# A two-layer adaptive-norm and expert network on one core: each step of the four middle stages gets its own place in its engine's order

## The chip, the core and the metric

One Trainium2 chip, of which one core is used. The metric is the device time of one execution of the whole program, in microseconds (us). Five engines each work through a list of instructions of their own, in the order in which the list was written: TensorE (PE in the profile; PEld is its weight load), VectorE (DVE), ScalarE (ACT), GpSimd (POOL) and SyncE (SP, which here only issues DMAs). An instruction that has to wait for a semaphore holds up everything behind it on its engine. So the order of each list is a large part of the program, and the change is one of order alone.

## What is computed

The input x is 8 x 256 tokens of 128 numbers. Two layers are applied, each with a residual; cut to what matters:

```python
x = x + L0_ffn(L0_cond(x, W1, b1, v, type_ids), gate_weight, w1, b1, w2, b2)
x = x + L1_ffn(L1_cond(x, language_ids, W1, b1, W2, b2, gamma, beta), ...)

# L0_cond: masked softmax pooling over a prefix, a postfix or all but one of the tokens
# L0_ffn: 8 experts, every token through every expert
kth_val = jnp.sort(logits.reshape(-1))[expert_k - 1]
gates = logits * (logits >= kth_val)
h = gelu_tanh(einsum('bld,ehd->bleh', x, w1) + b1)
out = einsum('bld e,ble->bld', einsum('bleh,edh->blde', h, w2) + b2.T, gates)

# L1_cond: adapter of the sample's language, then layernorm with its gamma and beta
h = relu(x @ W1[lang] + b1[lang]);  x = layernorm(x + h @ W2[lang] + b2[lang])
# L1_ffn: layernorm, softmax over 8 experts, the best 2 of them, exact gelu
w, idx = top_k(softmax(xn @ gate_w), 2);  w = w / sum(w)
output = sum over the 2 chosen experts of w * (gelu(xn @ w1[e] + b1[e]) @ w2[e] + b2[e])
return output + residual
```

The first expert layer is dense (8 experts for 2048 tokens, hidden width 512). The second is sparse: only 2 of 8 experts are computed for a token.

## The kernel before, in words

**Units.** The matmul work is cut into 88 units. Units 0 to 63 are dense (first layer): 16 steps of two (expert, group) parts, four hidden chunks each, where a group is 512 tokens (four groups, 0 to 3). Units 64 to 87 are pairs of tiles (second layer): a tile is 128 rows of tokens that chose one expert. Tiles 0 to 30 are batch 0 (tokens of groups 0, 1 and 2), tiles 31 to 45 are batch 1 (group 3). Each unit goes PE (first product, `pe_m1`, lines 533 to 562) to ACT (gelu, `act_gelu`, L627 and L632) to ACT (high half, `hi_part`, L649) to DVE (low half, `lo_part`, L656) to PE (second product, `pe_m2`, L596 and L597 for tiles, L606 to L608 for dense units). The operands are float16 in a high and a low half, so that each product is three matmuls.

**Gated sums.** For a dense result `gated` (L708, four instructions) adds it, times the gate, to the accumulator of its group. The gates come from a bisection of 12 rounds on DVE and PE (L1152 to L1193), and so the first ten results are kept in SBUF.

**Middle stages.** When a group's dense sums are complete, `mid(g)` (lines 1244 to 1580) takes it through 31 steps, each at its place among the units' instructions. In order of dependence, with the names of the table: `x1T` transpose on PE and `x1c` its copy on ACT; `h` and `hr`, `ad` and `xa`, the adapter; `st1`, `rs1`, `n1`, `x2`, the first layernorm (L1305 and L1310 statistics on DVE, L1329 and L1330 reciprocal root on POOL, L1338 and L1349 on DVE); `st2`, `rs2`, `n2`, `xn`, the second (L1362, L1370); `hi` (L1381) and `lo` (L1386) split the rows; `nT`, `nTc`, `lg`, the router's logits (L1393, L1400, L1408); `top`, the two best experts (L1419 to L1459); `tanh`, `wk`, their weights; `rk` and `rkd`, the rank of each row within its expert (L1522 to L1541, the last one writes the row addresses `idx`); `sc`, eight indirect DMAs on POOL (L1552) that scatter the group's rows to the DRAM buffer `sorted_in`; `gd`, `gT`, `gTc`, `b2m`, `b2x`, the bias of the second expert layer; `acc`, the residual (L728).

**Tiles.** When all groups of a batch are scattered and the tile table (L1605 to L1637) is there, SP loads each tile's rows (`sp_in`, L1662, with row addresses read from the table), PE transposes them (`pe_t`, L1692), ACT (batch 0) or DVE (batch 1) copies them out of PSUM, and DVE computes the rows' destination (`dve_xe`, L1727 and L1730). Results go through DVE (`dve_y`, L1718) and one indirect DMA for each tile on POOL (`pool_out`, L1669) to `sorted_out`. At the end SP loads the results back in token order and DVE adds them (`add_moe`, L746, four instructions for each group and choice), and SP stores (L1763).

**The order.** Every step is put into the list of its engine with a position, a number; each list is then sorted by it. Dense unit u stands at position 2u (a position is about 1.32 us), tile pairs `TILE` apart. A middle step's position is the group's start `M0[g]` plus an offset from the table `MID`, stretched by `SLACK`:

```python
def mid_pos(name, g):
    return M0[g] + (MID[name] + SLACK[g] * HOPS[name]) / UNIT_US
...
at("act", upos[u] + 0.7 * uwid[u], hi_part(u))
at("dve", upos[u] + 1.4 * uwid[u], lo_part(u))
...
at("dve", m2_pos(US + n, len(tiles) - 1) + 0.9, dve_y)
at("dve", mpos[("t", n)] + 0.8, dve_xe)
...
for q in Q.values():
    q.sort(key=lambda x: (x[0], x[1]))
```

`W16POS` says where the split of the second layer's weights into halves stands for each of the 8 experts (`w16_high` on ACT, L804, and `w16_low` on DVE, L811). In what follows a step of a group is written as name(group): `x2(2)` is the step `x2` of group 2.

Of the kernel before, what the change touches and what calls it, by code (L numbers as in the profile page):

```python
# [61 lines left out]
TILE = [1.45, 1.35]  # L62
GAP = 2.0
SLACK = [0.8, 0.8, 0.4, 0.0]

MID = {
# [17 lines left out]
W16POS = [3.0, 7.0, 11.0, 66.0, 71.0, 76.0, 81.0, 86.0]  # L84
# [3 lines left out]
def build_adaln_ffn(nc, t, out):  # L88
# [69 lines left out]
    with ExitStack() as ctx:  # L158
# [276 lines left out]
        M0 = [max(pos for pos, k, v in terms if group_of(k, v) == g) + 1.0 for g in range(NG)]
        M0[0] += 1.0
        M0[1] = max(M0[1], M0[0] + 9.0)
        M0[2] = max(M0[2], M0[1] + 7.0)
# [1487 lines left out]
```

## Time and profile before

| | |
|---|---|
| median of 3 runs | 424.14 us (422.88 to 426.02) |
| the profiled execution, its own time | 423.4 us |
| its span, first to last instruction | 421.6 us |
| mean granted TensorE clock | 0.908 |
| matmuls | 3474 |

The profile is of one execution. "Busy" is the time in which an engine runs an instruction. In a timeline row the first number is the start in us from the start of the span, the second how long the row lasts; "x4" means that four instructions are merged in it, and a bracket at the end gives the idle time of the engine ahead of it and who ended it. "issue" there means that nothing the profile shows ended the idle time. The granted clock is a share of full speed: 1.00 is 2.4 GHz, 0.50 is 1.2 GHz.

### The profile page before, as it was taken

To read this page: it belongs to the slowest core of one execution; us is meant where nothing else is said; L and a number is where in the kernel's file an instruction comes from. 1 tells how busy PE (TensorE), PEld (TensorE's weight loads), DVE (VectorE), ACT (ScalarE), POOL (GpSimd) and SP (SyncE) were. 2 spreads that over 40 slices of the span, in tenths; PEclk is the share of its full clock that TensorE was granted. 3 is DMA by queue.
4 is the path that set the end of the run, shared out by engine and by line. 5 is a ranking of instruction groups with operands and counts; after the bars stand their busy time and mean duration, and the time that the engine had idled before them with its cause. 6 is when DMAs were issued, how large, how long until landed. Compare 5 with 4: busy or idle time off the path is not lost.

```text
span 421.6 us, 9890 instructions
## 1 busy us (share of the span) xinstructions
PE 352.1 (84%) x3474; PEld 254.3 (60%) x3474; DVE 286.5 (68%) x796; ACT 241.9 (57%) x312; POOL 96.8 (23%) x100
## 2 busy tenths in 40 slices
PE   8988988999999998989579969149997898888920
PEld 5645865777776675757456647028675666666710
DVE  1754459988998666899978698513658844546672
ACT  3463287778887587987467656206355426633510
POOL 0000000000000000132146810700144577443440
PEclk9656699999999999999899998759988989999985
DMA  6892003326920203314001100121111222226132
GB/s 211 289 304 93 2 1 101 84 59 200 328 83 2 90 2 100 113 63 128 1 21 34 53 0 2 45 57 27 39 53 40 59 65 75 67 67 184 37 100 87
DMA packets 25762, 35.42 MB, mean 84 GB/s; under 512 B 6740, under 2 KB 21348, under 8 KB 25332
## 3 DMA queue, kind: packets, MB, share of 16 engines
q1 hardware_dynamic: 22900, 29.51, 23.7%
q0 software_dynamic: 2496, 5.15, 3.7%
q8 instruction: 30, 0.49, 0.5%
q10 hardware_dynamic: 320, 0.13, 0.1%
q14 instruction: 16, 0.13, 0.1%
HBM read 28.59 MB, written 15.64 MB: 105 GB/s over the span
## 4 chain that ended last, share of the span: by engine, by line
PE 44%; DVE 18%; issue 17%; POOL 10%; SPq 5%; DMA 4%; ACT 1%; POOLq 0%; DVEq 0%; ACTq 0%
POOL sorted_in L1552 4%; PE bank L606 4%; PE psA L559 4%; PE psA L561 4%; PE bank L607 4%; PE psA L560 4%; PE bank L608 4%; POOL sorted_out L1669 4%; DVE l L656 4%; PE bank L596 2%; DVE acc L708 2%; PE bank L995 2%; PE psA L544 2%; PE psA L540 2%; DVE w L811 2%
## 5 line engine op out<-in xcount | busy, mean ns | idle before, releaser
L656 DVE SCALAR_TENSOR_TENSOR l<-h 128x1024 f16<-128x1024 f32 x88 | 106.1, 1206 | 42.7 <-ACT h L649 42.5
L632 ACT ACTIVATE h<-psA,b1f 128x512 f32<-128x512 f32 (+1 forms) x96 | 76.0, 826 | 63.1 <-PE psA L561 62.6
L606 PE MATMUL bank<-w,h 128*128 128x128 f16 x512 | 92.7, 223 | 6.0 <-DVE acc L708 6.0
L649 ACT ACTIVATE h<-h 128x1024 f16<-128x1024 f32 x88 | 92.0, 1045 | 1.5
L607 PE MATMUL bank<-w,h 128*128 128x128 f16 x512 | 92.5, 223 | 0.0
L608 PE MATMUL bank<-w,l 128*128 128x128 f16 x512 | 92.4, 223 | 0.0
L1669 POOL DMA_INDIRECT sorted_out<-w,xe x46 | 46.9, 1019 | 77.5 <-DVE w L1718 35.7
L606 PEld LDWEIGHTS bank<-w,h 128*128 128x128 f16 x512 | 51.3, 100 | 17.0 <-DVE acc L708 9.7
L607 PEld LDWEIGHTS bank<-w,h 128*128 128x128 f16 x512 | 51.1, 100 | 6.0 <-issue 0.6
L627 ACT ACTIVATE h<-psA 128x1024 f32<-128x1024 f32 (+1 forms) x24 | 23.7, 988 | 53.4 <-PE psA L546 51.8
L608 PEld LDWEIGHTS bank<-w,l 128*128 128x128 f16 x512 | 51.2, 100 | 0.0
L1329 POOL TENSOR_SCALAR rs<-mv 128x4 f32<-128x4 f32 x8 | 4.6, 577 | 199.0 <-DVE mv L1310 198.9
L561 PE MATMUL psA<-xh,w 128*128 128x512 f16 x128 | 49.5, 387 | 0.0
L559 PE MATMUL psA<-xh,w 128*128 128x512 f16 x128 | 49.5, 386 | 0.0
L560 PE MATMUL psA<-xl,w 128*128 128x512 f16 x128 | 49.4, 386 | 0.0
L1552 POOL DMA_INDIRECT sorted_in<-pro,idx x32 | 35.6, 1113 | 37.5 <-DVE idx L1541 26.1
L596 PE MATMUL bank<-w,h 128*128 x184 | 34.5, 280 | 4.7 <-DVE l L656 3.6
L544 PE MATMUL psA<-wraw,w 128*128 128x128 f16 x184 | 36.3, 229 | 0.0
L546 PE MATMUL psA<-wraw,w 128*128 128x128 f16 x184 | 36.2, 228 | 0.0
L545 PE MATMUL psA<-wraw,w 128*128 128x128 f16 x184 | 35.9, 226 | 0.0
L597 PE MATMUL bank<-w,l 128*128 x184 | 32.7, 222 | 0.0
L708 DVE SCALAR_TENSOR_TENSOR acc<-bank,G,acc 128x128 f32<-128x128 f32 x88 | 24.4, 342 | 3.9 <-PE bank L608 3.7
(191 smaller groups left out, 570.8 us busy)
## 6 DMA issues: line engine op xcount, KB each, us to landing
sorted_in<-in_pad SPq DMA_DIRECT2D x8, 836.9 KB, 11.4
wraw<-in_w SPq DMA_DIRECT2D x10, 512.0 KB, 3.7
first<-sorted_in SPq DMA_DIRECT2D x46, 65.0 KB, 1.9
h<-in_w SPq DMA_DIRECT2D x5, 512.0 KB, 4.7
sorted_in<-in_pad SPq DMA_DIRECT2D x8, 316.9 KB, 4.6
w<-sorted_out SPq DMA_DIRECT2D x8, 256.0 KB, 3.7
mg<-in_maskt SPq DMA_DIRECT2D x8, 128.5 KB, 4.1
first<-in_xT SPq DMA_DIRECT2D x4, 256.0 KB, 4.5
```

What stands on the lines that cost most here:

```text
L544: pe.matmul(oo, w_h, a, start=False, stop=False, skip_group_check=True)
L559: pe.matmul(o[:, :], w_h, a, start=True, stop=False)
L560: pe.matmul(o[:, :], w_h, b_, start=False, stop=False)
L561: last = pe.matmul(o[:, :], w_l, a, start=False, stop=True)
L606: pe.matmul(oo, a, w_h, start=(c == 0 and k == 0), stop=False, skip_group_check=True)
L607: pe.matmul(oo, a, w_l, start=False, stop=False, skip_group_check=True)
L608: last = pe.matmul(oo, b_, w_h, start=False, stop=(c == 3 and k == 3), skip_group_check=True)
L632: last = act.activation(dst[:, q * w:q * w + w], src[:, q * w:q * w + w], ACT.Gelu_apprx_tanh, bias=b1f[:, es[q] * 4 + c:es[q] * 4 + c + 1 ...
L649: act.activation(wide(h16, h16_at[u], u), wide(h32, h32_at[u], u), ACT.Copy, scale=HS).then_inc(s_hi, 1)
L656: dve.scalar_tensor_tensor(wide(l16, h16_at[u], u), wide(h32, h32_at[u], u), HS, wide(h16, h16_at[u], u), ALU.mult, ALU.subtract).then_inc ...
L1552: pool.indirect_dma_start(scx[bt], bass.IndirectOffsetOnAxis(idx[:, g, k, i:i + 1], 0), xsf[:, 4 * (g % 2) + i, :], None).then_inc(t_sc[g] ...
L1669: pool.indirect_dma_start(scy[b], bass.IndirectOffsetOnAxis(xe[:, i:i + 1], 0), yo[:, yo_at(i), :], None)\
```

## The change

Computation, data, buffers, DMAs and their sizes stay as they are; only positions move. The formula for the middle steps becomes a table for each group (31 numbers each), the groups' starts come from `START`, and further positions come from `AT`. From the diff, cut:

```diff
-TILE = [1.45, 1.35]
-GAP = 2.0
-SLACK = [0.8, 0.8, 0.4, 0.0]
+TILE = [1.35, 1.35]
+GAP = 1.5
...
+    {"x1T": 0, "x1c": 0.65, "h": 4.01, "hr": 4.19, "ad": 5.77, "xa": 5.67, "st1": 7.81, "rs1": 6.58, "n1": 9.3, "x2": 11.08,
...
+START = [1.4, 10.5, 1, 2.5]
+AT = {"gate": 0.7, "hi": 0.95, "lo": 1.4, "m2d": 6.5, "m2t": 4.3, "m2s": 3.2, "t": 2.4, "tc": 0.7, "xe": -0.3, "y": 1,
+      "out": 1.35, "in": 9.4, "b2": 1.9, "moe0": -3.4, "moe1": 8, "moeg": 3, "moek": 0.95}
-KEPT = 1.5
+KEPT = 1.4
-W16POS = [3.0, 7.0, 11.0, 66.0, 71.0, 76.0, 81.0, 86.0]
+W16POS = [-1, 5, 11, 68, 71, 76, 81, 86]
...
-            return M0[g] + (MID[name] + SLACK[g] * HOPS[name]) / UNIT_US
+            return M0[g] + MID[g][name] / UNIT_US
...
-        MO = [tpos(NTL - 1) - 1.5, tpos(NTL - 1) + 8.0]
+        M0 = [max(pos for pos, k, v in terms if group_of(k, v) == g) + START[g] for g in range(NG)]
+        MO = [tpos(NTL - 1) + AT["moe0"], tpos(NTL - 1) + AT["moe1"]]
...
-                terms.append((MO[BATCH_OF[g]] + (1.5 * g if g < 3 else 0.0) + 0.7 * k, "moe", (g, k)))
+                terms.append((MO[BATCH_OF[g]] + (AT["moeg"] * g if g < 3 else 0.0) + AT["moek"] * k, "moe", (g, k)))
...
-            at("act", upos[u] + 0.7 * uwid[u], hi_part(u))
-            at("dve", upos[u] + 1.4 * uwid[u], lo_part(u))
+            at("act", upos[u] + AT["hi"] * uwid[u], hi_part(u))
+            at("dve", upos[u] + AT["lo"] * uwid[u], lo_part(u))
...
-            at("sp", tpos(i) - 7.0, sp_in)
+            at("sp", tpos(i) - AT["in"], sp_in)
...
-            at("dve", m2_pos(US + n, len(tiles) - 1) + 0.9, dve_y)
-            at("dve", mpos[("t", n)] + 0.8, dve_xe)
+            at("dve", m2_pos(US + n, len(tiles) - 1) + AT["y"], dve_y)
+            at("dve", mpos[("t", n)] + AT["xe"], dve_xe)
```

The changed file is five lines longer in the part of the middle stages and the tiles, so L1349 before is L1354 after.

What it comes to in the lists, at the three places that the prediction speaks of. The first is DVE from `x2(2)` to `xn(2)`. Before (L1349 is `x2`, L1305 and L1310 are `st2`, L1362 is `n2`, L728 is `acc`, L1370 is `xn`, L656 a unit's low half, L736 the bias of group 1):

```order
L1349 SCALAR_TENSOR_TENSOR pro<-pro,rs,mg 128x128 x4
L656 SCALAR_TENSOR_TENSOR l<-h 128x1024
L1305 BN_STATS st<-pro 128x6 x4
L736 TENSOR_TENSOR acc<-acc,bank 128x4x128
L1310 BN_AGGR mv<-st 128x2 x4
L1362 SCALAR_TENSOR_TENSOR pro<-pro,mv,fgb 128x128 x4
L656 SCALAR_TENSOR_TENSOR l<-h 128x1024
L728 TENSOR_TENSOR acc<-acc,pro 128x4x128
L1370 SCALAR_TENSOR_TENSOR pro<-pro,rs,fgb 128x128 x4
```

The same place after:

```order
L1354 SCALAR_TENSOR_TENSOR pro<-pro,rs,mg 128x128 x4
L1310 BN_STATS st<-pro 128x6 x4
L1315 BN_AGGR mv<-st 128x2 x4
L661 SCALAR_TENSOR_TENSOR l<-h 128x1024
L1367 SCALAR_TENSOR_TENSOR pro<-pro,mv,fgb 128x128 x4
L733 TENSOR_TENSOR acc<-acc,pro 128x4x128
L1375 SCALAR_TENSOR_TENSOR pro<-pro,rs,fgb 128x128 x4
```

The statistics now follow `x2` at once; of two low halves one stands in the stretch, and group 1's bias is gone from it.

The second is POOL from the scatter of group 2 on. Before (L1552 is a scatter, L1669 the output of a tile, L1329 and L1330 `rs1(3)` and then `rs2(3)`):

```order
L1552 DMA sorted_in<-pro,idx 13184x130 x8
L1669 DMA sorted_out<-w,xe 16256x128 x6
L1329 TENSOR_SCALAR rs<-mv 128x4
L1330 TENSOR_TENSOR rs<-rs,mhalf 128x4
L1669 DMA sorted_out<-w,xe 16256x128 x2
L1329 TENSOR_SCALAR rs<-mv 128x4
L1330 TENSOR_TENSOR rs<-rs,mhalf 128x4
L1669 DMA sorted_out<-w,xe 16256x128 x6
L1552 DMA sorted_in<-pro,idx 4992x130 x8
L1669 DMA sorted_out<-w,xe 16256x128 x17
```

The same place after:

```order
L1557 DMA sorted_in<-pro,idx 13184x130 x8
L1674 DMA sorted_out<-w,xe 16256x128 x6
L1334 TENSOR_SCALAR rs<-mv 128x4
L1335 TENSOR_TENSOR rs<-rs,mhalf 128x4
L1674 DMA sorted_out<-w,xe 16256x128 x6
L1334 TENSOR_SCALAR rs<-mv 128x4
L1335 TENSOR_TENSOR rs<-rs,mhalf 128x4
L1674 DMA sorted_out<-w,xe 16256x128 x8
L1557 DMA sorted_in<-pro,idx 4992x130 x8
L1674 DMA sorted_out<-w,xe 16256x128 x11
```

The scatter of group 3 stood behind 14 tile outputs and stands behind 20.

The third is DVE near the end. Before (L746 is `add_moe` of batch 0, L1718 is `dve_y`, L1710 copies the last pair's turned rows, L1727 and L1730 are `dve_xe`, L656 a low half):

```order
L656 SCALAR_TENSOR_TENSOR l<-h 128x1024
L1718 TENSOR_REDUCE w<-bank 128x256
L1710 COPY wraw<-bank 128x256
L1727 TENSOR_TENSOR xk<-first,tef 128x1
L1730 SCALAR_TENSOR_TENSOR xe<-xk,first 128x1
L746 SCALAR_TENSOR_TENSOR acc<-w,wk,acc 128x128 x12
L656 SCALAR_TENSOR_TENSOR l<-h 128x1024
L1718 TENSOR_REDUCE w<-bank 128x256
L746 SCALAR_TENSOR_TENSOR acc<-w,wk,acc 128x128 x4
L656 SCALAR_TENSOR_TENSOR l<-h 128x512
L746 SCALAR_TENSOR_TENSOR acc<-w,wk,acc 128x128 x8
L1718 TENSOR_REDUCE w<-bank 128x256
```

The same place after:

```order
L751 SCALAR_TENSOR_TENSOR acc<-w,wk,acc 128x128 x4
L1732 TENSOR_TENSOR xk<-first,tef 128x1
L1735 SCALAR_TENSOR_TENSOR xe<-xk,first 128x1
L661 SCALAR_TENSOR_TENSOR l<-h 128x1024
L751 SCALAR_TENSOR_TENSOR acc<-w,wk,acc 128x128 x4
L1723 TENSOR_REDUCE w<-bank 128x256
L1715 COPY wraw<-bank 128x256
L751 SCALAR_TENSOR_TENSOR acc<-w,wk,acc 128x128 x4
L661 SCALAR_TENSOR_TENSOR l<-h 128x1024
L1723 TENSOR_REDUCE w<-bank 128x256
L751 SCALAR_TENSOR_TENSOR acc<-w,wk,acc 128x128 x4
L661 SCALAR_TENSOR_TENSOR l<-h 128x512
```

The three additions that stood in one block ahead of the low half of unit 86 are spread, the first of them ahead of the low half of unit 85.

Further moves that the prediction names: the split of expert 0's and 1's weights (`w16_low`) stands on DVE ahead of the start of the bisection, which it followed or interrupted; on PE `nT(2)` stands ahead of both parts of the second product of unit 55 instead of behind them, `lg(2)` ahead of the first product of unit 59 instead of behind the second of unit 56, `rk(2)` ahead of the first product of unit 60 instead of behind the second product of unit 58, and `gT(2)` between the two parts of that one, which was behind the transpose of tiles 0 and 1; `rk(1)` stands on PE ahead of the first product of unit 52 instead of behind the second product of unit 49; `rk(3)` stands within unit 73's second product instead of ahead of unit 72's first product.

## Rows read from the trace of the kernel before

**Rows 1.** The page: engines, busy us (share of the span) and instructions
```profile
PE 352.1 (84%) x3474; PEld 254.3 (60%) x3474; DVE 286.5 (68%) x796; ACT 241.9 (57%) x312; POOL 96.8 (23%) x100
```

**Rows 2.** The page: busy tenths in 40 slices of 10.5 us, and PE's granted clock
```profile
PE   8988988999999998989579969149997898888920
...
DVE  1754459988998666899978698513658844546672
...
PEclk9656699999999999999899998759988989999985
```

**Rows 3.** Stretches: us, then busy us (instructions) of PE, PEld, DVE, ACT, POOL; clock; DMA
```profile
280.00:290.00 10.00, 9.70 (x79) 6.44 (x78) 3.53 (x7) 4.78 (x7) 0.00 (x0) 0.70 0.24 55
...
297.00:343.00 46.00, 40.06 (x396) 29.98 (x394) 32.03 (x117) 20.06 (x28) 21.51 (x23) 0.90 0.17 47
```

**Rows 4.** Timeline of DVE at the start of the bisection
```profile
63.42 1.22 DVE L811 SCALAR_TENSOR_TENSOR w<-wraw,w 128x1024 f16<-128x1024 f32 x1
64.56 0.16 DVE L1058 COPY L<-bank 128x16 f32<-128x16 f32 x1
```

**Rows 5.** Timeline of PE: the two waits of the middle of the program
```profile
250.94 0.63 PE L1393 MATMUL bank<-ident,pro 128*128 128x128 f32 x4 [3.85 <-DVE pro L1370]
...
279.85 0.37 PE L1692 MATMUL bank<-identh,first 128*128 128x128 f16 x2 [15.15 <-DMA first<-sorted_in]
```

**Rows 6.** Timeline of POOL: group 0's first scatter, 1's last, 2's first and last
```profile
215.34 2.00 POOL L1552 DMA_INDIRECT sorted_in<-pro,idx  x1 [10.64 <-DVE idx L1541]
...
240.45 0.95 POOL L1552 DMA_INDIRECT sorted_in<-pro,idx  x1 [0.30 <-issue]
...
263.94 1.34 POOL L1552 DMA_INDIRECT sorted_in<-pro,idx  x1 [15.51 <-DVE idx L1541]
...
273.18 0.96 POOL L1552 DMA_INDIRECT sorted_in<-pro,idx  x1 [0.31 <-issue]
```

**Rows 7.** Timeline of DVE: group 2 from x2 to its row addresses
```profile
242.90 1.14 DVE L1349 SCALAR_TENSOR_TENSOR pro<-pro,rs,mg 128x128 f32<-128x128 f32 x4 [3.59 <-issue]
...
246.47 0.37 DVE L1310 BATCH_NORM_AGGREGATE mv<-st 128x2 f32<-128x6 f32 x4
...
249.66 1.13 DVE L1370 SCALAR_TENSOR_TENSOR pro<-pro,rs,fgb 128x128 f32<-128x128 f32 x4
...
262.99 0.17 DVE L1541 CAST idx<-pk 128x8 uint32<-128x8 f32 x1
```

**Rows 8.** The chain that ended last, start and us: from the scatters to the rows
```profile
275.79 1.85 SPq L506
278.36 2.12 DMA first<-sorted_in
```

**Rows 9.** Timeline of PE: the three waits for steps of group 3
```profile
307.65 1.13 PE L1289 MATMUL bank<-cw,hTs 33*128 33x128 f32 x8 [0.96 <-ACT hTs L1282]
...
323.53 1.08 PE L1393 MATMUL bank<-ident,pro 128*128 128x128 f32 x4 [1.84 <-DVE pro L1370]
...
338.08 0.29 PE L1492 MATMUL bank<-ident,b2d 128*32 128x128 f32 x1 [2.62 <-DVE tei L1637]
```

**Rows 10.** Timeline of ACT: gelu of two tile pairs that follow each other
```profile
360.68 1.02 ACT L627 ACTIVATE h<-psA 128x1024 f32<-128x1024 f32 x1 [1.63 <-PE psA L546]
...
364.80 1.02 ACT L627 ACTIVATE h<-psA 128x1024 f32<-128x1024 f32 x1 [1.67 <-PE psA L546]
```

**Rows 11.** Timeline of POOL and PE: end of group 3's scatter, batch 1's first transpose
```profile
346.61 1.37 POOL L1552 DMA_INDIRECT sorted_in<-pro,idx  x1 [0.31 <-issue]
...
369.40 0.38 PE L1692 MATMUL bank<-identh,first 128*128 128x128 f16 x4 [1.92 <-issue]
```

**Rows 12.** Timelines of DVE and PE near the end
```profile
398.74 3.37 DVE L746 SCALAR_TENSOR_TENSOR acc<-w,wk,acc 128x128 f32<-128x128 f32 x12
402.02 1.22 DVE L656 SCALAR_TENSOR_TENSOR l<-h 128x1024 f16<-128x1024 f32 x1
...
403.49 0.28 PE L596 MATMUL bank<-w,h 128*128 x1 [2.82 <-DVE l L656]
```

More of the change, by code:

```diff
@@ L61 @@
 UNIT_US = 1.32
-TILE = [1.45, 1.35]
-GAP = 2.0
-SLACK = [0.8, 0.8, 0.4, 0.0]
-MID = {
[4 rows of a table removed]
-}
-HOPS = {
[3 rows of a table removed]
-}
-KEPT = 1.5
+TILE = [1.35, 1.35]
+GAP = 1.5
+MID = [
[16 rows of a table added]
+]
+START = [1.4, 10.5, 1, 2.5]
+AT = {"gate": 0.7, "hi": 0.95, "lo": 1.4, "m2d": 6.5, "m2t": 4.3, "m2s": 3.2, "t": 2.4, "tc": 0.7, "xe": -0.3, "y": 1,
+      "out": 1.35, "in": 9.4, "b2": 1.9, "moe0": -3.4, "moe1": 8, "moeg": 3, "moek": 0.95}
+KEPT = 1.4
 W0HI = [-99.0, -98.0, -97.0, -96.0, -95.0, -38.2, -36.2, -34.4]
@@ L140, in build_adaln_ffn @@
     for u, q in M2:
-        p = max(p + 0.45, upos[u] + ((4.3 if UNITS[u][0] == "tile" else 6.5) + 0.5 * q if uwid[u] == 2 else 3.2 if UNITS[u][0] == "tile" else 4.2))
+        p = max(p + 0.45, upos[u] + (AT["m2t" if UNITS[u][0] == "tile" else "m2d"] + 0.5 * q if uwid[u] == 2 else AT["m2s"]))
         m2_at[(u, q)] = p
@@ L425, in build_adaln_ffn @@
             else:
-                pos = m2_pos(last_unit[x[:2]], x[2]) + 0.7
+                pos = m2_pos(last_unit[x[:2]], x[2]) + AT["gate"]
             terms.append((pos, "y", x))
@@ L430, in group_of @@
             return STEPS[v[1]][v[2]][1] if kind == "y" else (v[0] if kind == "moe" else v)
-        b2_pos = [max(PG + 1.5 + KEPT * ND, 0) + 1.0 + 0.9 * g for g in range(NG)]
+        b2_pos = [max(PG + 1.5 + KEPT * ND, 0) + 1.0 + AT["b2"] * g for g in range(NG)]
         for g in range(NG):
             terms.append((b2_pos[g] + 0.6, "b2", g))
[L435 to L438, printed above, removed]
-        MO = [tpos(NTL - 1) - 1.5, tpos(NTL - 1) + 8.0]
+        M0 = [max(pos for pos, k, v in terms if group_of(k, v) == g) + START[g] for g in range(NG)]
+        MO = [tpos(NTL - 1) + AT["moe0"], tpos(NTL - 1) + AT["moe1"]]
         for g in range(NG):
@@ L472, in build_adaln_ffn @@
         for n in range(NP):
-            misc.append((upos[US + n] - 2.4, ("t", n), (t_xt, n + 1)))
+            misc.append((upos[US + n] - AT["t"], ("t", n), (t_xt, n + 1)))
         misc.sort(key=lambda x: x[0])
@@ L1673, in pe_register @@
                 tile_register(pe, "pe", i)
-            at("sp", tpos(i) - 7.0, sp_in)
+            at("sp", tpos(i) - AT["in"], sp_in)
             if n % LOADS == 0:
                 at("pe", mpos[("t", pair_of[i])] - 0.05, pe_register)
-            at("pool", m2_pos(u, last) + 1.5, pool_out)
+            at("pool", m2_pos(u, last) + AT["out"], pool_out)
         def tile_pair(n):
@@ L1731, in dve_xe @@
                                          xrf[:, i:i + k, D + 1:D + 2], ALU.mult, ALU.add).then_inc(t_xe, 1)
-            at("dve", m2_pos(US + n, len(tiles) - 1) + 0.9, dve_y)
-            at("dve", mpos[("t", n)] + 0.8, dve_xe)
+            at("dve", m2_pos(US + n, len(tiles) - 1) + AT["y"], dve_y)
+            at("dve", mpos[("t", n)] + AT["xe"], dve_xe)
             at("pe", mpos[("t", n)], pe_t)
             if b == 0:
-                at("act", mpos[("t", n)] + 0.7, act_x)
+                at("act", mpos[("t", n)] + AT["tc"], act_x)
             else:
-                at("dve", mpos[("t", n)] + 0.7, dve_x)
+                at("dve", mpos[("t", n)] + AT["tc"], dve_x)
         for i in range(NTL):
```

22 rows, old and new, of tables (HOPS, MID) are left out of this document.

## The prediction

> **What bounds the kernel now.** Start with the engines' line [rows 1]: PE is busy for 352 us of 421.6, no other engine for more than 68%. So time can only be won where PE stands idle or runs at a low clock, and the 40 slices [rows 2] say where: PE is nearly full from slice 8 to slice 19, has holes from slice 20 to 27 (down to 1 in slice 26), and ends in a slice of 2 and one of 0. The granted clock falls in the same places. In the first stretch PE itself is the bound, and an earlier middle step buys nothing.
>
> Next the waits of PE. The largest stands at 279.85 [rows 5]: 15.15 us, until the rows of the first tile have landed. Behind it on PE are a dense unit and all the tiles, so what shortens that wait moves everything after it. Follow it back. The last scatter of group 2 begins at 273.18, the first at 263.94 [rows 6]; after the last come the landing, SP's read of the row addresses (275.79, 1.85 us) and the load (278.36, 2.12 us) [rows 8]. The scatter begins when DVE has written the addresses, `idx(2)`, at 262.99 [rows 7]. Before that stand `xn(2)` at 249.66, for which PE waits 3.85 us [rows 5, 7], and `x2(2)` at 242.90, for which DVE sat idle 3.59 us [rows 7]: it needs `rs1(2)` of POOL, and POOL scattered group 1 until 240.45 + 0.95 [rows 6]. So this is one chain from group 1's scatter to the first tile, DVE and POOL by turns, and PE has slack beside it: 15 us.
>
> In the tile stage PE waits three times for steps of group 3: 0.96, 1.84 and 2.62 us [rows 9], and its clock in 297 to 343 us is 0.90 [rows 3]. Two levels of 1.00 and 0.50 give 0.90 when 20% of the 46 us, 9.2 us, are at the low one; the work in them took up to twice as long, so up to 4.6 us are lost to the clock. At the end, three additions in one block (398.74, 3.37 us) hold up the low half of unit 86, and PE waits 2.82 us for it [rows 12].
>
> **The change part by part.** No instruction is added or removed, so every term is a wait that goes or comes.
>
> A, start of the bisection. `w16_low` of expert 0 (1.14 us from its start at 63.42 to the next instruction's at 64.56 [rows 4]) stands ahead of the copy of the last logits. It goes to a place where DVE waits for PE. The bisection's first matmul and the unit behind it start that much earlier, and PE is full from there on, so it lasts. Value -1.1 us; bounds 0 (the logits are late anyway) and -1.1.
>
> B, the chain to the first tile. Group 0's steps stand earlier on PE, ACT and DVE; this fills idle time of DVE ahead of 171 us, and its addresses come some 1.8 us earlier, worked out step by step in the new order with the durations of the old rows, so its scatter starts at about 213.5 instead of 215.34 [rows 6]. `rk(1)` no longer waits for the first product of unit 52 and what stands around it; `idx(1)` gains about 4 us. Group 1's scatter is then bound by group 0's, and ends at about 237.5 instead of 241.4: -3.9, and `x2(2)` with it. From `x2(2)` to `xn(2)` it was 249.66 - 242.90 = 6.76 us [rows 7]; in the new order DVE has five pieces there after `x2` itself, statistics 0.87 + 0.38, a low half 1.14, `n2` 1.05, `acc` 0.60, with `x2` 1.05: 5.1 us, -1.7. From `xn(2)` to `idx(2)` it was 262.99 - 249.66 = 13.3 us [rows 7]; one low half (1.14) leaves this stretch: -1.1. The sum is -6.7. I take -5.9, since three stops of PE (2 to 4 us each, at `nT(2)`, `rk(2)` and `gT(2)`) are now in front of dense units, and a low half that the ranks wait for may come later at the low clock. These stops cost nothing by themselves: the dense work behind them is 13 us, and the slack was 15.15. Bounds: -1.7 (only the order from `x2` to `xn` counts) and -8.
>
> On the stops, the row at 279.85 [rows 5] and the stretch after it at a clock of 0.70 [rows 3] show that PE comes out of a wait at 1.2 GHz. The Trainium skill, page TensorE: Matmul & The Clock Gate, section "HAM oscillation — how this bites in real kernels", says that a PE which is starved again and again restarts cold each time, and this speaks against B: by it all of the dense work after `nT(2)` runs at half speed, 26 us instead of 13. By my steps even that ends about when the first rows land, so the sum would be the same within a microsecond; the trace agrees with the rule as far as the 0.70 goes.
>
> C, dense units under the first tiles. `gT(2)` leaves the place behind the first transpose and the first product of unit 66 goes ahead of a second product that waited for a gated sum. -2.0; bounds 0 and -2.5.
>
> D, group 3 in the tile stage. Its 31 steps are spread over about 12 pairs instead of 9. `xn(3)` on DVE stands a whole pair ahead of `nT(3)` on PE and the logits a pair after that. The three waits are 0.96 + 1.84 + 2.62 = 5.4 us [rows 9], with up to 4.6 of clock [rows 3]: 10.0. I take -7.0, as some of the clock's share lies at the first tiles, which stay. Bounds -3 and -10.
>
> E, the hand-over to batch 1. This is what the spreading spends. Group 3's scatter stands behind six more outputs on POOL. Before, it ended at 346.61 + 1.37 = 348.0 and the first transpose of batch 1 was at 369.40 [rows 11]: 21 us of slack. Now count from U, the end of unit 73's second product on PE, to which both sides hang. The rows of batch 1: `dve_y` and its hand-over 0.9, two outputs 2.5, and from a group's first scatter to the first transpose 279.85 - 263.94 = 15.9 us [rows 5, 6], in which landing, SP's read and the load are contained [rows 8]: 19.3 us. PE asks for them after 4 pairs of 364.80 - 360.68 = 4.1 us [rows 10], some 1.4 for `gT(3)` and `b2m(3)`, 1.1 for a read of expert addresses and 1.2 for a half pair: 20.1 us. Nearly a tie: 0 us; bounds 0 and +8.
>
> F, the end. The three additions in a block are spread; the low half of unit 86 comes 1.1 us earlier and the last `dve_y` pairs 1.5 to 1.9. -1.5; bounds 0 and -2. What follows the last output is the same DMA, load, four additions and store.
>
> The positions of the gated sums, the biases of layer 0, SP's DMAs and GAP I cost at nothing: between 77 and 159 us PE has no idle time for them to fill, which slices 8 to 15 [rows 2] show, and each keeps its place relative to the unit that waits for it. If that cover were gone, a gated sum is 1.1 us.
>
> Sum: -1.1 - 5.9 - 2.0 - 7.0 + 0 - 1.5 = -17.5. The profiled execution took 423.4 us, so 405.9; the median of the runs is 0.7 higher, so 406.6, and I say 407.
>
> **The rivals.** First, the hand-over binds. For it: the margin of E is 0.8 us, and scatters differ (1.34 and 0.96 us within one group [rows 6]). Against it: any other stop of PE before batch 1 widens the margin. If D is won, but the rows of batch 1 come late by all of it, D is given back: 414.
>
> Second, the chain is given back. DVE is busy 7 to 9 tenths in slices 17 to 22 [rows 2], so an instruction put early puts another late. Then B keeps only its lower bound and what hangs on it: -1.1 - 1.7 - 2.0 - 7.0 - 1.5 = -13.3, and if C goes too, -11.3: 412.
>
> Third, the change does not do what it says: waits move and none goes, as each list has the same work. Against it is that PE idles 15 us at one place for a chain that has gaps of its own (3.59, 3.85). 424.
>
> Fourth, the other sign: group 3's steps still stop a pair each. From 297 to 343 us PE has 396 matmuls [rows 3]; a pair has 46 and group 3 some 28, so eight pairs took 46 us, 5.75 each, against 4.1 later [rows 10]. If they keep that cadence, and for twelve pairs instead of nine, that is 3 x 1.65 = +5. The scatter's slack of 21 us is gone all the same, and with scatters like the first of group 0 (2.00 us [rows 6]) and a low clock after the wait the hand-over is late by its bound, +8. With A, the lower bound of B, and C (-4.8), none of D and F: +8, so 432. It begins at group 3's adapter, the first row of rows 9, and decides the sign when cadence and hand-over together cost more than the 4.8 us.
>
> **How the numbers follow.** My forecast 0.60, the hand-over 0.19, the chain given back 0.10, no effect 0.06, slower 0.05. The range: the forecast with D and B at their far bounds is 407 - 3.0 - 2.1 = 402, and I go to 400 for what may have gone elsewhere; upward it takes in the two rivals at 412 and 414 with 4 us for the bound of E: 418. Within 1% is within 4.2 us, about what a measurement of this kernel can tell from no change. Faster by over 1% holds the first three, 0.89; within 1% is 0.06; slower 0.05.
>
> **What would show it.** A: the first count of the bisection on PE near 64.2 instead of 65.3. B: `rs1(2)` near 236, `idx(2)` near 256, the first tile's transpose near 273, and its wait 6 us or less, with up to three waits of 2 to 4 us ahead of it. D: no wait of PE for group 3 over 1 us, and a clock over 0.95 in the first twelve pairs. E: the wait before batch 1's first transpose at 0 to 3 us; 5 or more means the first rival. F: no 2.8 us wait at the second product of unit 86. Wrong would be a first transpose at 278 or later (B), or pairs that still take 6 us with group 3 beside them (D).

## The result, and the profile after

| | before | after |
|---|---|---|
| median of 4 runs, us | 424.14 (422.88 to 426.02) | 408.31 (406.11 to 413.05) |
| profiled execution, us | 423.4 | 407.57 |
| its span, us | 421.6 | 405.8 |

The ratio after to before is 0.961, with a 95% interval from 0.954 to 0.967. Predicted were 407 us, in a range from 400 to 418. The medians are of all runs; the ratios, here and below, leave out runs over 1.5% above the fastest of their kernel, such as the one of 413.05 us.

Since every step keeps its name, the two executions can be laid beside each other at four steps of PE. This table is used for every kernel below: the first count of the bisection; from it to the first tile's transpose; on to batch 1's first transpose (tile 31); on to the next pair's; and from there to the end of the span. The times up to the first count differ by up to 3 us between executions, with no edit there but term A's, and are left out of the readings. Each row of such a table is one execution. Where kernels have the same places for groups 0 to 2 and the same offsets (after, `mid3_old` and `sc3_again` below), the second column repeats within 0.3 us.

| us | first count | to tile 0 | to tile 31 | to the next pair | to the end |
|---|---|---|---|---|---|
| before | 65.31 | 214.55 | 89.55 | 4.41 | 47.79 |
| after | 63.95 | 210.29 | 80.13 | 5.58 | 45.84 |
| difference | -1.36 | -4.26 | -9.42 | +1.17 | -1.95 |

The differences add up to -15.8, the whole gain of the span. More than half lies in the tiles of batch 0, beside group 3's steps.

The page of after: the engines' line, and of the 40 slices (10.1 us each) those of PE and DVE:

```profile
PE 352.7 (87%) x3474; PEld 252.2 (62%) x3474; DVE 286.5 (71%) x796; ACT 241.4 (59%) x312; POOL 102.1 (25%) x100
...
PE   8888989999999999998699978659999999798930
...
DVE  1654468988999567899998778534448787356772
```

PE's busy time is that of [rows 1] within 1 us; what went is idle time. In [rows 2] PE had a hole down to 1 tenth in slice 26; now the lowest slice of the middle is a 5 (slice 27), and slices 28 to 34 are all 9 where some had 7 or 8. The same two stretches as [rows 3], in after:

```profile
280.00:290.00 10.00, 10.00 (x135) 8.38 (x133) 2.72 (x5) 4.77 (x6) 0.00 (x0) 0.87 0.08 18
297.00:343.00 46.00, 43.01 (x483) 32.25 (x481) 34.06 (x121) 27.20 (x37) 27.86 (x27) 1.00 0.21 57
```

In the 46 us PE runs 483 matmuls instead of 396, at a granted clock of 1.00 instead of 0.90. The waits of [rows 9] are down to 0.5 us and less each. Next the waits ahead of the first tile, in the timeline of PE:

```profile
243.98 0.63 PE L1398 MATMUL bank<-ident,pro 128*128 128x128 f32 x4 [3.42 <-DVE pro L1375]
...
255.71 0.19 PE L1525 MATMUL bank<-OB,triu 128*128 128x32 bf16 x1 [2.54 <-DVE cumb L1464]
...
265.56 0.37 PE L1497 MATMUL bank<-ident,b2d 128*32 128x128 f32 x1 [3.56 <-DVE b2d L1492]
...
274.25 0.27 PE L1697 MATMUL bank<-identh,first 128*128 128x128 f16 x2 [3.47 <-DMA first<-sorted_in]
```

These are `nT(2)`, `rk(2)`, `gT(2)` and the first tile. The wait of 15.15 us of [rows 5] has become four of 3 us: the chain is 4.3 us shorter, and the rest of the idle time now stands among the dense units. Two more of its links, the timeline of POOL (group 1's scatter and `rs1(2)`, group 2's first transfer) and that of DVE:

```profile
223.37 0.95 POOL L1557 DMA_INDIRECT sorted_in<-pro,idx  x1 [0.74 <-issue]
224.63 0.95 POOL L1557 DMA_INDIRECT sorted_in<-pro,idx  x1 [0.30 <-issue]
225.89 1.54 POOL L1557 DMA_INDIRECT sorted_in<-pro,idx  x1 [0.30 <-issue]
227.73 0.95 POOL L1557 DMA_INDIRECT sorted_in<-pro,idx  x1 [0.30 <-issue]
228.99 1.96 POOL L1557 DMA_INDIRECT sorted_in<-pro,idx  x1 [0.30 <-issue]
...
233.78 2.28 POOL L1557 DMA_INDIRECT sorted_in<-pro,idx  x1 [0.30 <-issue]
236.08 0.26 POOL L1334 TENSOR_SCALAR rs<-mv 128x4 f32<-128x4 f32 x1
...
257.73 1.10 POOL L1557 DMA_INDIRECT sorted_in<-pro,idx  x1 [15.39 <-DVE idx L1546]
```

```profile
225.37 1.23 DVE L661 SCALAR_TENSOR_TENSOR l<-h 128x1024 f16<-128x1024 f32 x1 [2.52 <-ACT h L654]
...
228.90 1.21 DVE L661 SCALAR_TENSOR_TENSOR l<-h 128x1024 f16<-128x1024 f32 x1
...
232.96 1.14 DVE L1343 SCALAR_TENSOR_TENSOR pro<-pro,mv,mg 128x128 f32<-128x128 f32 x4
234.01 1.22 DVE L661 SCALAR_TENSOR_TENSOR l<-h 128x1024 f16<-128x1024 f32 x1
237.56 1.14 DVE L1354 SCALAR_TENSOR_TENSOR pro<-pro,rs,mg 128x128 f32<-128x128 f32 x4 [2.33 <-issue]
...
242.70 1.13 DVE L1375 SCALAR_TENSOR_TENSOR pro<-pro,rs,fgb 128x128 f32<-128x128 f32 x4
...
254.07 1.23 DVE L661 SCALAR_TENSOR_TENSOR l<-h 128x1024 f16<-128x1024 f32 x1 [1.62 <-ACT h L654]
255.21 0.35 DVE L1464 TENSOR_TENSOR cumb<-cumb,OB 128x8 bf16<-128x8 bf16 x2
...
256.78 0.17 DVE L1546 CAST idx<-pk 128x8 uint32<-128x8 f32 x1
```

`x2(2)` to `xn(2)` is now 5.1 us (6.8 in [rows 7]), but `xn(2)` to `idx(2)` 14.1 (13.3): the last additions for the ranks (255.21) stand behind a low half that waits 1.62 us for ACT, and `rk(2)` on PE, which its new place puts ahead of two dense units, waits with them. At the hand-over to batch 1:

```profile
354.37 0.37 PE L1697 MATMUL bank<-identh,first 128*128 128x128 f16 x2 [2.00 <-DMA first<-sorted_in]
```

And at the end the single wait of 2.82 us of [rows 12] is two:

```profile
388.16 0.28 PE L601 MATMUL bank<-w,h 128*128 x1 [1.02 <-DVE l L661]
...
390.41 0.28 PE L601 MATMUL bank<-w,h 128*128 x1 [0.76 <-DVE l L661]
```

### The profile page after: what moved, and what is told of

Read it like the earlier page. It is cut to its first block, busy times and chain, and to the rows that moved or that the text cites. A ratio compares the mean times of both kernels' runs of the same rounds, so it can differ in the third digit from the quotient of the medians.

```text
span 405.8 us, 9890 instructions
## 1 busy us (share of the span) xinstructions
PE 352.7 (87%) x3474; PEld 252.2 (62%) x3474; DVE 286.5 (71%) x796; ACT 241.4 (59%) x312; POOL 102.1 (25%) x100
## 4 chain that ended last, share of the span: by engine, by line
PE 49%; DVE 14%; issue 14%; POOL 10%; SPq 6%; DMA 5%; ACT 2%; POOLq 0%; DVEq 0%; ACTq 0%
POOL sorted_in L1557 5%; PE bank L611 5%; PE psA L564 5%; PE psA L565 5%; PE psA L566 5%; PE bank L613 5%; PE bank L612 5%; POOL sorted_out L1674 3%; DVE l L661 3%; PE bank L1000 3%; PE bank L601 2%; PE psA L549 1%; PE psA L545 1%; PE bank L1021 1%; DMA sorted_in<-pro,idx 1%
## 5 line engine op out<-in xcount | busy, mean ns | idle before, releaser
L613 PE MATMUL bank<-w,l 128*128 128x128 f16 x512 | 93.4, 224 | 0.0
L1674 POOL DMA_INDIRECT sorted_out<-w,xe x46 | 48.1, 1045 | 62.8 <-DVE xe L1735 27.4
L565 PE MATMUL psA<-xl,w 128*128 128x512 f16 x128 | 50.7, 396 | 0.0
L564 PE MATMUL psA<-xh,w 128*128 128x512 f16 x128 | 50.6, 395 | 0.0
L566 PE MATMUL psA<-xh,w 128*128 128x512 f16 x128 | 50.5, 395 | 0.0
L1557 POOL DMA_INDIRECT sorted_in<-pro,idx x32 | 37.8, 1181 | 34.7 <-DVE idx L1546 25.1
L549 PE MATMUL psA<-wraw,w 128*128 128x128 f16 x184 | 34.4, 223 | 0.0
L551 PE MATMUL psA<-wraw,w 128*128 128x128 f16 x184 | 34.0, 220 | 0.0
L550 PE MATMUL psA<-wraw,w 128*128 128x128 f16 x184 | 33.9, 220 | 0.0
## 6 DMA issues: line engine op xcount, KB each, us to landing
sorted_in<-in_pad SPq DMA_DIRECT2D x8, 836.9 KB, 13.3
```

The costliest lines, as they stand in the source:

```text
L564: pe.matmul(o[:, :], w_h, a, start=True, stop=False)
L565: pe.matmul(o[:, :], w_h, b_, start=False, stop=False)
L566: last = pe.matmul(o[:, :], w_l, a, start=False, stop=True)
L613: last = pe.matmul(oo, b_, w_h, start=False, stop=(c == 3 and k == 3), skip_group_check=True)
L1557: pool.indirect_dma_start(scx[bt], bass.IndirectOffsetOnAxis(idx[:, g, k, i:i + 1], 0), xsf[:, 4 * (g % 2) + i, :], None).then_inc(t_sc[g] ...
L1674: pool.indirect_dma_start(scy[b], bass.IndirectOffsetOnAxis(xe[:, i:i + 1], 0), yo[:, yo_at(i), :], None)\
```

## The experiments

The theory is that of the prediction, with the sizes of the table: the gain is a sum of separate terms, B (the chain to the first tile) by the order of the middle stages, D by spreading group 3, A and F by themselves. The rivals: the pace, loads and offsets carry it and not the tables of the middle stages; or the terms eat each other up at the hand-over to batch 1. Each ratio is against runs of before that were made beside the kernel's own.

**1. The middle stages alone, and all but them.** `mids_old` is after with

```diff
-    {"x1T": 0, "x1c": -0.8, "h": 1.9, "hr": 2.7, "ad": 4.2, "xa": 5.6, "st1": 5.6, "rs1": 7.1, "n1": 7.2, "x2": 8.9,
...
+    {"x1T": 0, "x1c": 0.3, "h": 1.9, "hr": 2.9, "ad": 4.6, "xa": 5.6, "st1": 6.4, "rs1": 7.9, "n1": 8, "x2": 9.3,
...
-START = [1.4, 10.5, 1, 2.5]
+START = [2.0, 10.5, 1, 1.0]
```

(row 3 is shown; each of the four is the old `MID[name] + SLACK[g] * HOPS[name]`) and with `"xe": 0.8`. `only_mids` keeps the new rows and starts and takes the rest back (the line of `AT` that is left out takes back `hi`, `xe` and `y`):

```diff
-TILE = [1.35, 1.35]
-GAP = 1.5
+TILE = [1.45, 1.35]
+GAP = 2.0
...
-      "out": 1.35, "in": 9.4, "b2": 1.9, "moe0": -3.4, "moe1": 8, "moeg": 3, "moek": 0.95}
+      "out": 1.5, "in": 7.0, "b2": 0.9, "moe0": -1.5, "moe1": 8, "moeg": 1.5, "moek": 0.7}
...
-KEPT = 1.4
+KEPT = 1.5
...
-W16POS = [-1, 5, 11, 68, 71, 76, 81, 86]
+W16POS = [3.0, 7.0, 11.0, 66.0, 71.0, 76.0, 81.0, 86.0]
```

> The changed kernel with all four middle stages back at their old places (one table with a slack, old starts); the w16 casts, pace of the tile units, loads, unit offsets and first batch's additions keep their new places (the first sorting column of the tiles, xe, goes back to +0.8, since it must stand behind the table of tiles). Theory (the gain is the sum of separate terms, and the chain of group 2 and the spread of group 3 carry most of it): only the start of the bisection (1.1 us) and the end (1.5 to 2 us) are left, so 420 to 422 us. Rival (the new pace, loads and offsets carry the gain and the tables only fit them): 408 to 413 us.

> The kernel before with the new tables of the four middle stages and their new starts, and nothing else of the change. Theory: 1.1 us of the bisection's start and 1.5 to 2 us of the end are missing, 411 to 412 us. Rival (tables need the new pace of the tile units and the earlier row loads): 416 us or more, with the first tile's transpose not before 277 us or the stops of group 3 back.

Measured: `mids_old` 418.03 us (ratio 0.987, 0.979 to 0.995), `only_mids` 409.3 us (0.963, 0.957 to 0.969).

| us | first count | to tile 0 | to tile 31 | to the next pair | to the end |
|---|---|---|---|---|---|
| mids_old | 64.31 | 213.57 | 86.97 | 5.29 | 46.16 |
| only_mids | 65.21 | 207.87 | 83.16 | 4.44 | 47.72 |

The tables of the middle stages alone bring 14.6 of the 15.8 us, so the first rival falls. What is left without them, 5.9 us, is more than I said (2.6 to 3.1): 2.6 us of it lie in the tiles of batch 0. Both kernels were faster than I expected, and their gains together are 20.5 us, not 15.8: the terms are not separate as the theory has it. By the table most of the excess, 3.4 us, stands up to tile 0, where the tables alone bring 6.7 us, the rest alone 1.0, and both together 4.3. A and F are there as expected: with the rest of the change and without the tables, the last column falls by 1.6, and with the tables alone by 0.1. A slow stretch of the clock behind tile 31 can fall into either of the last two columns, so they are safest read as a sum: 52.2 us before, 51.4 after, 51.4 in `mids_old`, 52.2 in `only_mids`. One number was unexpected: `only_mids` comes to tile 0 2.4 us sooner than after does. That is the scatter of group 1, and comes below.

**2. One group at a time.** `mid3_old` takes back row 3 as above and its start; `mid2_old` takes back row 2, with `"xe": 0.8`:

```diff
-START = [1.4, 10.5, 1, 2.5]
+START = [1.4, 10.5, 1, 1.0]
```

```diff
-    {"x1T": 0, "x1c": 0.65, "h": 4.01, "hr": 4.19, "ad": 5.77, "xa": 5.67, "st1": 7.81, "rs1": 6.58, "n1": 9.3, "x2": 11.08,
...
+    {"x1T": 0, "x1c": 0.7, "h": 2.7, "hr": 4.1, "ad": 6.2, "xa": 7.6, "st1": 8.4, "rs1": 10.3, "n1": 10.4, "x2": 12.1,
...
```

> The changed kernel with group 3's row of the table and its start back at their old places. Theory (term D: group 3's steps come in one clump and hold DVE, each stop of TensorE costing itself and a slower clock after it): nothing changes up to the first tile (274 us), group 3's stops of 1 to 2.6 us come back, the last unit of the first batch ends 6 to 9 us later, 414 to 417 us. Rival (the tiles run better because TensorE comes into them with less held up and xe, the sorting column, earlier, not because of group 3's places): 408 to 410 us.

> The changed kernel with group 2's row of the table back at its old places (and xe at +0.8). Theory (term B is mostly set by when group 1's scatter ends and by x2 to idx of group 2): group 1's scatter still ends near 237.5 us and group 2's first rstd follows it, the first tile's transpose moves from 274 to 275.5 to 278 us, total 409.5 to 412.5 us. Rival (all of B is group 2's own order): the first transpose near 280 us and 414 us or more.

Measured: `mid3_old` 413.73 us (0.974, 0.967 to 0.982), `mid2_old` 408.77 us (0.960, 0.953 to 0.968).

| us | first count | to tile 0 | to tile 31 | to the next pair | to the end |
|---|---|---|---|---|---|
| mid3_old | 63.91 | 210.30 | 87.06 | 3.79 | 47.45 |
| mid2_old | 66.78 | 207.71 | 79.95 | 7.76 | 46.49 |

Group 3's places are 6.9 us in the tiles of batch 0 and nothing before them, as term D said; by the medians the kernel loses 5.4 us without them. The stretch in `mid3_old`, to be read beside the one of after (43.01 us of PE in x483, clock 1.00):

```profile
297.00:343.00 46.00, 40.57 (x413) 29.29 (x411) 31.93 (x115) 21.88 (x30) 26.91 (x27) 0.93 0.21 57
```

Group 2's own row is worth nothing in the total, and with the old row tile 0 comes 2.6 us sooner. That was a miss of my expectation. PE of `mid2_old` waits only 0.87 us for `nT(2)` and not at all for `rk(2)` and `gT(2)` ahead of the tiles, but since PE of after, with its stops, still waits 3.47 us for the first rows, these stops don't set when tile 0 comes. What does is group 1's scatter: it begins 159.4 us after the first count in both kernels, and takes 10.2 instead of 12.7 us:

```profile
229.97 0.95 POOL L1557 DMA_INDIRECT sorted_in<-pro,idx  x1 [0.30 <-issue]
231.23 0.96 POOL L1557 DMA_INDIRECT sorted_in<-pro,idx  x1 [0.30 <-issue]
232.49 1.33 POOL L1557 DMA_INDIRECT sorted_in<-pro,idx  x1 [0.30 <-issue]
234.13 0.96 POOL L1557 DMA_INDIRECT sorted_in<-pro,idx  x1 [0.30 <-issue]
235.39 0.96 POOL L1557 DMA_INDIRECT sorted_in<-pro,idx  x1 [0.30 <-issue]
236.38 0.25 POOL L1334 TENSOR_SCALAR rs<-mv 128x4 f32<-128x4 f32 x1
```

`only_mids` confirms it: with group 2's new places, but a scatter of 10.1 us, it comes to tile 0 as soon as `mid2_old` (207.87 and 207.71). So what is lost is not the new places as such, but how the scatter meets DVE's work.

In after three of its eight transfers took 1.54, 1.96 and 2.28 us; here the longest takes 1.33. In the rows of DVE above, the first two start while DVE makes a low half (225.37 and 228.90). The third starts at 233.78, within the last instruction of `n1(2)` (232.96), which a low half (234.01) follows at once, and it ends 0.83 us after that low half. What `mid2_old` wins before the tiles it loses at the hand-over: the next pair after tile 31 comes 7.76 us later instead of 5.58, as tile 31 waits for its rows and the clock is at 0.80 in the 25 us around it:

```profile
354.44 0.37 PE L1697 MATMUL bank<-identh,first 128*128 128x128 f16 x2 [2.81 <-DMA first<-sorted_in]
```

```profile
350.00:375.00 25.00, 20.18 (x196) 14.68 (x193) 11.03 (x22) 9.79 (x12) 13.72 (x14) 0.80 0.36 101
```

**3. The hand-over to batch 1.** After waits 2.00 us at tile 31, put down to the rows, and `idx(3)` is ready 3.6 us ahead of the scatter. `sc3_early` moves that scatter one pair of outputs forward on POOL:

```diff
-     "acc": 19.2, "top": 23.2, "tanh": 25.1, "wk": 26.1, "rk": 27.2, "rkd": 27.9, "sc": 30.7, "gd": 30.3, "gT": 31.3,
+     "acc": 19.2, "top": 23.2, "tanh": 25.1, "wk": 26.1, "rk": 27.2, "rkd": 27.9, "sc": 28.64, "gd": 30.3, "gT": 31.3,
```

> The changed kernel with group 3's scatter one pair of tile outputs earlier on GpSimd (row 3, sc 30.7 to 28.64), since its indices are ready at 334.96 us and it starts at 338.54, behind four outputs. Theory (term E was not 0: the changed kernel reaches tile 31's transpose 2.0 us before its rows are there, and the slower clock after that stop costs 1.3 us more): the scatter ends 2.5 us earlier, the stop goes, 404.5 to 406 us. Rival (the hand-over binds nothing, the outputs that go later hold VectorE and the banks instead): 408 us or more.

In the first set of runs in which it stood (with `rs1_early`, `g01_old` and `best1`) before itself took 438.55 us. Engines stood idle there at two places with nothing in the profile of the core that released them: in `rs1_early`, for one, DVE for 11.0 us and ACT for 9.9 us ahead of 362 us, while PE ran 14 matmuls in 10 us. So the ratios of that set, 0.968 to 0.971, tell nothing apart, and all but `rs1_early` were run again.

> The kernel of sc3_early once more, since in its own set of runs every kernel, the one before too, stood still for several us at two places with nothing to release them. Theory (the hand-over of batch 1 costs the changed kernel 3.3 us: 2.0 of waiting, 1.3 of the slower clock after it): group 3's scatter ends near 346.4 us, 2.5 us earlier, no wait for rows is left ahead of tile 31, 404.5 to 406 us where before is at 424. Rival (the hand-over binds nothing, or outputs that go later hold VectorE and the banks instead): 408 us or more.

Measured: 407.11 us (0.959, 0.953 to 0.965): the same as after. The scatter ended at 347.36 instead of 348.92, 2.3 us earlier counted from the first count. Tile 31 came as late as in after, 290.7 and 290.4 us from the first count:

```profile
355.43 0.48 PE L1697 MATMUL bank<-identh,first 128*128 128x128 f16 x3 [2.12 <-issue]
```

The time lies between the two ranges that I gave; the trace decides for the rival, that the hand-over binds nothing. The wait of 2 us stays and only changes its name: it is PE's own read of the expert addresses, a TENSOR_LOAD of its sequencer (L511) that takes 2.02 us from 352.19 in after and 2.16 us from 353.10 here. The wait of 1.92 us in [rows 11] stands behind the same read, 1.95 us. The rows land just within it: the hand-over in after is the tie that the prediction worked out. The slower clock behind this stop (5.58 us to the next pair, 5.33 here, 4.41 before) doesn't come from the rows either. Nor does it come from the spread of group 3: `only_mids`, with the new tables, has 4.44 us and, like before, a clock of 1.00 from 4 us ahead of tile 31 to its last matmul, and `mids_old`, with the old tables, has 5.29. All eight undisturbed traces with the new pace and offsets have a stretch at the lower clock there. Which of these positions brings it, I leave open.

**4. GpSimd's order ahead of group 2.** `rs1_early` puts `rs1(2)` behind the fifth transfer of group 1's scatter (`"rs1": 6.58` to `5.86` in row 2); `g01_old` and `g01_again`, one kernel, take rows 0 and 1 and group 0's start back:

```diff
-    {"x1T": 0, "x1c": 0.1, "h": 2.9, "hr": 4.5, "ad": 7, "xa": 8.8, "st1": 9.6, "rs1": 13.4, "n1": 12.2, "x2": 14.1,
...
+    {"x1T": 0, "x1c": 1.1, "h": 3.5, "hr": 5.3, "ad": 7.8, "xa": 9.6, "st1": 10.4, "rs1": 12.7, "n1": 12.8, "x2": 14.9,
...
-START = [1.4, 10.5, 1, 2.5]
+START = [2.0, 10.5, 1, 2.5]
```

> The changed kernel with group 2's first rstd on GpSimd set behind the fifth of the eight transfers of group 1's scatter instead of behind all (row 2, rs1 6.58 to 5.86). Its input is ready at 230.4 us, it starts at 236.08. Theory (this wait is on the chain that sets the first tile): rstd near 231 us, x2 2.3 us earlier, the first tile's transpose 1.5 to 2.5 us earlier, 405.5 to 407 us. Rival (the chain is paced by VectorE's and TensorE's order behind it, not by this rstd): the first transpose within 0.7 us of before, 408 us.

It ran only in the disturbed set (426.86 us, before 438.55), which doesn't decide it. `best2` below has this move together with others, so its share alone is not measured.

> The kernel of g01_old once more: groups 0 and 1 at their old places. Theory (when group 1's scatter ends sets group 2's first rstd, and through it the first tile: with it group 2's own row of the table, which alone changed nothing, explains term B): the scatter ends 3.5 to 4 us later, counted from the first count of the bisection, the first tile's transpose 3 to 4 us later, total 411 to 412.5 us where before is at 424. Rival (group 2's new places take up a late scatter, so that no row of the table has a share of its own): first transpose less than 1.5 us later, 408 to 410 us.

Measured: 417.95 us (0.985, 0.979 to 0.990), 5.5 to 7 us more than I expected.

| us | first count | to tile 0 | to tile 31 | to the next pair | to the end |
|---|---|---|---|---|---|
| g01_again | 64.97 | 217.05 | 81.86 | 6.95 | 45.97 |

Timeline of POOL, where the addresses of group 1's scatter were ready at 228.5:

```profile
235.21 0.23 POOL L1334 TENSOR_SCALAR rs<-mv 128x4 f32<-128x4 f32 x1 [8.07 <-DVE mv L1315]
235.52 1.05 POOL L1335 TENSOR_TENSOR rs<-rs,mhalf 128x4 f32<-128x4 f32 x1
236.76 1.10 POOL L1557 DMA_INDIRECT sorted_in<-pro,idx  x1 [0.19 <-issue]
...
248.98 0.25 POOL L1334 TENSOR_SCALAR rs<-mv 128x4 f32<-128x4 f32 x1
```

The new `rs1(2)` and the old `sc(1)` have changed places in the list: POOL waits 8.07 us for group 2's statistics, and the whole scatter waits behind it; then `rs2(2)` waits for the scatter. So this kernel does not measure rows 0 and 1 alone. It shows that the rows fit only each other: `mids_old` to `mid2_old` (rows 0, 1, 3 changed, row 2 old in both) is 213.57 to 207.71, -5.9 us up to tile 0, and that is the share of rows 0 and 1, as row 3 has none there.

**5. Put together.** `best1`: row 2 old but for `"rs1": 5.86`. `best2`: row 2 new up to the logits with `"rs1": 5.86`, from there on near the old places:

```diff
-     "acc": 14.62, "top": 22.19, "tanh": 22.59, "wk": 26.84, "rk": 22.53, "rkd": 25.58, "sc": 29.06, "gd": 28.47,
-     "gT": 26.69, "gTc": 29.74, "b2m": 30.82, "b2x": 33.32},
+     "lo": 18.32, "lg": 19.9, "acc": 14.62, "top": 21.5, "tanh": 23.2, "wk": 25.2, "rk": 23.9, "rkd": 26.2, "sc": 27.9,
+     "gd": 27.7, "gT": 30.6, "gTc": 31.4, "b2m": 33, "b2x": 34.9},
```

Both have group 3's `"sc": 28.64` and `"xe": 0.8`.

> The kernel of best1 once more: group 3's scatter one pair of outputs earlier, group 2's first rstd in the midst of group 1's scatter, the rest of group 2 at its old places. Theory (first tile and hand-over both cost, and the two gains add up): first transpose 2 us or more earlier than in the changed kernel counted from the first count of the bisection, 402 to 405 us where before is at 424. Rival (the chain behind the rstd is paced elsewhere, and only the hand-over's part is gained): 405.5 to 408 us.

> Group 2 at the new places up to its logits, with its first rstd in the midst of group 1's scatter (its input is then ready at 230.4 us; with the old places it was not, and best1 gained nothing by it), and from the logits on near the old places (the new ones put the rank ahead of two dense units, where it waited 2.5 us for VectorE); group 3's scatter one pair of outputs earlier. Theory (the chain from group 2's statistics to its scatter sets the first tile at each of its links): first transpose 3.5 to 4.5 us earlier than in the changed kernel counted from the first count, 402 to 404.5 us. Rival (the links give back what the one ahead gains, since VectorE is in order): no better than best1, 405 to 407 us.

Measured: `best1` 404.92 us (0.952, 0.945 to 0.959), `best2` 403.77 us (0.952, 0.946 to 0.958).

| us | first count | to tile 0 | to tile 31 | to the next pair | to the end |
|---|---|---|---|---|---|
| best1_again | 64.47 | 207.80 | 79.08 | 5.88 | 46.48 |
| best2 | 64.39 | 206.13 | 79.38 | 5.67 | 46.02 |

`best1` keeps the 2.5 us of `mid2_old` up to tile 0 and pays less at the hand-over (5.88 instead of 7.76). Its early `rs1(2)` gave nothing, because with the old places its input wasn't ready. In `best2` it was:

```profile
229.36 1.95 POOL L1557 DMA_INDIRECT sorted_in<-pro,idx  x1 [0.30 <-issue]
231.34 0.25 POOL L1334 TENSOR_SCALAR rs<-mv 128x4 f32<-128x4 f32 x1
...
238.05 1.11 POOL L1334 TENSOR_SCALAR rs<-mv 128x4 f32<-128x4 f32 x1 [0.37 <-DVE mv L1315]
```

`rs1(2)` runs 4.7 us earlier than in after (231.34 instead of 236.08), and tile 0 comes 4.2 us sooner counted from the first count. Of these, 2.5 us are there at `x2(2)`, 0.6 come between `xn(2)` and `idx(2)`, and 1.2 from group 2's scatter, which takes 10.0 instead of 11.15 us. Against `only_mids`, whose group 1 scatter DVE didn't hold up, tile 0 gains 1.7. The theory's range held in both kernels. Both medians lie 3.4 and 4.5 us below the one of after, though the intervals of the ratios still touch.

## Why the prediction was right

**A** was -1.1 and measured -1.1: of the 1.36 us in the table 0.22 lie ahead of the edit. The first count came at 63.95 (said: near 64.2).

**B** was -5.9 and measured -4.3; its mechanism was right and two links were mis-sized. Group 1's scatter was to end 3.9 us earlier and did, by 4.0 (236.06 instead of 241.40, less the 1.36 of the start). `x2(2)` to `xn(2)` was to be 1.7 shorter and is 1.6. "From `xn(2)` to `idx(2)` ... one low half (1.14) leaves this stretch: -1.1" is the step that failed: the stretch became 0.75 longer, since the ranks' last additions stand behind a low half that waits for ACT. I had named this mishap, and the 0.8 us that I took off the sum of 6.7 for it and the stops were too few. And group 2's scatter, for which I had no term, is longer: its eight transfers took 11.15 us instead of 10.20. -4.0 - 1.6 + 0.75 + 0.95 is -3.9; 0.35 more was won between scatter and rows. `mid2_old` shows the cost of my taking the whole chain as gained: row 2 of the table alone brings nothing in the total. And the end of group 1's scatter was right in part by luck: counted from the first count it starts 5.5 us earlier than before, more than the 4 that I had, and takes 12.7 instead of 11.2 us, which I had not foreseen.

The stops that I forecast ahead of the first tile are there in number and size (3.42, 2.54, 3.56, then 3.47 for the tile). Between 244 and 271 us the granted clock is 0.75, and the dense work behind `nT(2)` ends at 270.8 instead of 13 us after it. The Trainium skill's rule of a PE that restarts cold each time (page TensorE: Matmul & The Clock Gate, section "HAM oscillation — how this bites in real kernels"), by which this work would take 26 us, is borne out only in part: a mean of 0.75 is half of the time at each of the two levels, not all of it at the lower one, and the total of 27 us comes near 26 only because 6.7 us of waits are in it. As the prediction said, it cost nothing: the rows came later still.

**C and D** were -2.0 and -7.0 and measured -9.4 together. `mid3_old` splits them: group 3's places are 6.9, the rest 2.5. That this is near C's 2.0 is in part luck, as half of C's mechanism is not it: `mids_old`, with `gT(2)` at its old place, gains 2.6 in the same column, and `only_mids`, with `gT(2)` moved, 6.4, which is no more than D. The other half is there, but small: before and `only_mids` have a wait of PE of 0.75 us for a gated sum, some 16 us behind the first tile, and after and `mids_old` don't. The rest of the 2.5 goes with the pace and the offsets, and isn't located. Said were no wait for group 3 over 1 us and a clock above 0.95; the largest is 0.5, the clock 1.00.

**E** was 0 with a bound of +8. The rows and PE meet within the 2 us of the address read (I had put it at 1.1), which is the tie worked out from U, and `sc3_again` shows that an earlier scatter changes nothing. But +1.2 us are there, behind the stop: the clock of 0.93 between 350 and 375 us, which I had not counted. It goes with the new pace and offsets, which I had costed at nothing, and not with the spread of group 3; its cause isn't shown.

**F** was -1.5 and measured -1.95; PE's two waits for low halves at the end went from 3.6 to 1.8 us in sum.

The sum -1.1 - 4.3 - 9.4 + 1.2 - 2.0 is -15.6, with 0.2 of the start -15.8; forecast were -17.5, and the whole difference is B's 1.6 and E's 1.2, less what C and D (0.4), F (0.5) and the start (0.2) won more. So errors of both signs cancelled in part. Of the rivals, "the hand-over binds" does not hold for after but for `mid2_old`, by 2.2 us: whoever shortens the chain further meets it. "The chain is given back" holds for 1.6 of 5.9 us.

## What to carry to other kernels

In an order written by hand, price an early place not only by the step it hurries but by the in-order neighbour that then waits: in `g01_again` an early `rs1(2)` held GpSimd for 8 us ahead of a scatter, and tile 0 came 6.8 us later than in after. An early `rk(2)` held PE for 2.5 us in after and cost nothing, since PE had slack there. A wait's name is the last releaser, not the only one: before moving a transfer for it, look for a second reason of equal length, as PE's address read was here. And test the parts of a table of places together with their neighbours, since a row taken back alone can turn two entries around.

## What the runs showed of the hardware

A GpSimd indirect transfer takes 0.96 us on its engine when DVE is idle: of 342 that started so in the ten traces outside the disturbed set, none took over 1.10. One that starts while DVE makes a low half (1.22 us, two inputs in SBUF) takes up to 2.1, and one that started in the instruction ahead of a low half took 2.3. Of all 780 transfers 138 started within such an instruction, and 115 of them ended 0.78 to 0.90 us after its end. Of the other 23, 15 ended up to 1.08 us after it, and 8 that started with it, within 0.04 us, weren't held. In the other 642 the median is 0.96, and 32 took over 1.2. So the transfer is held until DVE is through, and then needs 0.83 us. What DVE does matters, not only that it is busy: of 130 transfers that started while DVE ran an instruction with an operand in PSUM, none took over 1.10. In after this made group 1's scatter 12.7 us long where 10.1 are possible (`only_mids`, 10.1, with the same rows of the table), and I had taken the 2.00 and 1.34 us of [rows 6] for chance.

The Trainium skill (SBUF — State Buffer, section "🔬 SBUF: two separate sides") states that DVE and GpSimd have one pair of ports between them that is locked for a whole instruction, and that a transfer issued by GpSimd can be kept from writing its descriptors in this way. It says the latter of DVE instructions in a two-port mode; for those with two inputs in SBUF it has the lock only against a GpSimd instruction that reads SBUF. The traces agree in that the transfer waits for the end of the DVE instruction, here one with two inputs in SBUF; that the ports are the reason, no run shows.
